# Cross attention with 16 heads: scores on two row tiles of 64 rows, rows built through memory

## The reference

```python
h = layernorm(x)                                   # [8, 256, 128]
q, k, v = split(h @ w_qkv.T)                       # 16 heads of 8 features
k = concat([context_k, k]);  v = concat([context_v, v])   # 512 + 256 = 768 keys
attn = softmax((q * 8 ** -0.5) @ k.T)              # per head [256, 768], fp32
x = x + (attn @ v) @ w_proj.T + b_proj
x = x + expert_ffn(layernorm(x))                   # 8 experts, 2 per row
```

## Time and profile before

| | us |
|---|---|
| median of 3 runs (lowest, highest) | 581.93 (579.75, 582.76) |
| the profiled execution, its own time | 579.1 |
| its span, first to last instruction | 577.5 |
| TensorE / VectorE / ScalarE / GpSimd busy | 498.9 / 353.9 / 292.7 / 196.0 |

### The profile page before, as it was taken

One profiled execution on the slowest core, in us unless ns is written; L12 is line 12 of the kernel. 1 busy time (PEld: TensorE's weight loads), 2 busy tenths in 40 slices (PEclk: granted clock), 3 DMA queues, 4 the chain that ended last, 5 costly groups with the idle time before them and its releaser, 6 DMA issues. The chain is left out here.

```text
span 577.5 us, 10586 instructions
## 1 busy us (share of the span) xinstructions
PE 498.9 (86%) x3467; PEld 322.9 (56%) x3468; DVE 353.9 (61%) x646; ACT 292.7 (51%) x584; POOL 196.0 (34%) x381
## 2 busy tenths in 40 slices
PE   3479999999999999999999998555499999999940
PEld 1346666666666666666565663244447666666630
DVE  7597687777777787777777770368524333333316
ACT  2136667767767677676776767421023333333310
POOL 7151241331422412411400000103317776677630
PEclk9999999999999999999999999865569999999995
DMA  6802434445244344342332300160101111111116
GB/s 168 185 25 72 94 88 108 95 105 134 75 113 121 87 120 104 91 115 64 76 72 58 90 3 2 36 184 0 14 10 43 41 41 38 39 36 43 42 51 189
DMA packets 32078, 44.39 MB, mean 77 GB/s; under 512 B 5484, under 2 KB 20460, under 8 KB 32036
## 3 DMA queue, kind: packets, MB, share of 16 engines
q1 hardware_dynamic: 27076, 36.88, 25.7%
q0 software_dynamic: 2560, 5.25, 3.6%
q10 hardware_dynamic: 2400, 1.70, 1.2%
HBM read 16.58 MB, written 4.72 MB: 37 GB/s over the span
## 5 line engine op out<-in xcount | busy, mean ns | idle before, releaser
L426 DVE TENSOR_REDUCE max_part<-max_ps 128x2 f32<-128x1024 f32 (+1 forms) x192 | 231.3, 1221 | 79.6 <-PE max_ps L519 42.1
L385 ACT ACTIVATE probs<-exp_ps 128x512 f32<-128x512 f32 x384 | 207.4, 591 | 77.5 <-PE exp_ps L541 72.0
L541 PE MATMUL exp_ps<-blocks,keys 128*128 128x512 f32 x384 | 160.9, 421 | 4.5 <-ACT probs L385 2.3
L519 PE MATMUL max_ps<-keys,blocks 128*128 128x512 f32 x256 | 109.9, 436 | 10.1 <-DMA blocks<-masked 7.0
L541 PEld LDWEIGHTS exp_ps<-blocks,keys 128*128 128x128 f32 x384 | 71.7, 187 | 44.8 <-ACT probs L385 18.5
L551 PE MATMUL pv_ps<-probs,value_cols 128*32 128x256 f32 x1536 | 96.3, 383 | 0.0
L986 DVE TENSOR_TENSOR hidden<-up_ps,silu 128x512 f32<-128x512 f32 x40 | 27.7, 692 | 84.4 <-PE up_ps L1076 82.4
L302 POOL CAST maxes<-rowmax 128x8 fp32r<-128x8 f32 x32 | 6.3, 198 | 178.6 <-DVE rowmax L432 178.6
L519 PEld LDWEIGHTS max_ps<-keys,blocks 128*128 128x128 f32 x256 | 48.4, 191 | 30.2 <-DVE max_part L426 19.2
L551 PEld LDWEIGHTS pv_ps<-probs,value_cols 128*32 128x32 f32 x1536 | 43.3, 109 | 39.4 <-issue 17.1
L879 ACT ACTIVATE hiddenT<-at_ps 128x512 f32<-128x512 f32 x40 | 23.9, 597 | 77.2 <-PE at_ps L1093 68.7
(11 more groups left out here) (148 smaller groups left out, 473.4 us busy)
## 6 DMA issues: line engine op xcount, KB each, us to landing
blocks<-masked SPq DMA_DIRECT2D x93, 128.0 KB
keys<-parts SPq DMA_DIRECT2D x96, 96.0 KB
ctx_v_sb<-ctx_v_dram SPq DMA_DIRECT2D x8, 256.0 KB, 2.9
gate<-gateT_dram SPq DMA_DIRECT2D x8, 256.0 KB, 2.8
up<-upT_dram SPq DMA_DIRECT2D x8, 256.0 KB, 2.6
y_in<-pick_outs SPq DMA_DIRECT2D x8, 256.0 KB, 4.9
raw<-ctx_kT_dram SPq DMA_DIRECT2D x7, 256.0 KB, 2.8
h_rows<-h SPq DMA_DIRECT2D x4, 256.0 KB, 4.9
```

The source lines that it names most:

```text
L385: act.activation(probs[par][:, k, 2 * half:2 * half + 2], exp_ps[u % 2][:].rearrange("p (g n) -> p g n", n=N), ACT.Exp).then_inc(exp_done, 1)
L426: vec.reduce_max(out, bank, axis=AX.X).then_inc(max_done, 1)
L519: mm = pe.matmul(max_ps[w % 2][:, half * BANK:(half + 1) * BANK], blocks[:, t, w, half * P:(half + 1) * P], keys[:, t, 0:NC_], start=True, ...
L541: pe.matmul(exp_ps[u % 2][:], keys[:, t, k * P:(k + 1) * P], blocks[:, t, 2 * half:2 * half + 2, :], start=True, stop=True).then_inc(exp_f ...
```

## The change

`keys` and `blocks` are laid out for two pairs of heads a quad. Pair a = 0 lies on partitions 0 to 49 and pair a = 1 on 64 to 113: three bands of 16 rows each (2 heads of 8 features) and two sum rows. A matmul takes 64 partitions (maxima: 48) in place of 128, and matmuls of the two pairs stand on different row tiles of the array. The number of score matmuls and their columns stay the same. In each group both halves of the maxima unit come first (a = 1, then a = 0), and then the exponential units for a = 0 and a = 1, each with a PSUM bank of its own. The maxima matmuls leave the sum rows out, so the clearing DMA goes.

SP writes the bands of a whole batch to DRAM by six DMAs (`write_bands`), and reads those of a quad back by four (`read_bands`). `parts` and `masked` have one buffer each in place of two. `masked`, its making and `blocks` are half as wide. The sum rows of a quad take two DMAs in place of one.

```diff
+PAIR = G // 2
+TILE = P // 2
+BAND = PAIR * D
+MAX_ROW = 3 * BAND
...
-        masked = sb("masked", [P, 2, 2, G, N])
+        masked = sb("masked", [P, 2, PAIR, N])
-        blocks = sb("blocks", [P, T, G, N], F32R)
+        blocks = sb("blocks", [P, T, PAIR, N], F32R)
+        key_bands = nc.dram_tensor("key_bands", (2, 2 * T, 3, BAND, KEYS), F32, kind="Internal").ap()
+        query_bands = nc.dram_tensor("query_bands", (2, 2 * T, 3, BAND, PAIR * N), F32, kind="Internal").ap()
...
-            def spread_rows(q):
+            def write_bands(c):
+                if c >= 2:
+                    for t in range(T):
+                        sp.wait_ge(rows_in[t], rows_spread(T * (c - 2)))
+                for j, part in enumerate((0, 1, 0)):
+                    sp.dma_start(key_bands[c % 2, :, j], parts_f[:, part, 0:KEYS]).then_inc(bands_in[c % 2], 16)
+                for j, part in enumerate((0, 0, 1)):
+                    sp.dma_start(query_bands[c % 2, :, j], masked[:, part]).then_inc(bands_in[c % 2], 16)
+
+            def read_bands(q):
                 c, t = divmod(q, T)
...
+                sp.wait_ge(bands_in[c % 2], bands_written(c))
+                for a in range(2):
+                    rows = slice(TILE * a, TILE * a + MAX_ROW)
+                    sp.dma_start(blocks_f[rows, t], query_bands[c % 2, 2 * t + a].rearrange("j i n -> (j i) n"))\
+                      .then_inc(rows_in[t], 16)
+                    sp.dma_start(keys_f[rows, t], key_bands[c % 2, 2 * t + a].rearrange("j i n -> (j i) n"))\
                       .then_inc(rows_in[t], 16)
...
-            sp.wait_ge(blocks_zero, T)
             sp.wait_ge(ctx_split, 2)
-            sp.wait_ge(own_first, 2)
-            spread_rows(0)
             sp.wait_ge(own_first, 4)
-            for q in range(1, T):
-                spread_rows(q)
+            write_bands(0)
+            sp.wait_ge(blocks_zero, 1)
+            sp.wait_ge(rows_const, 1)
+            for q in range(T):
+                read_bands(q)
...
                     sp.wait_ge(maxT_copied, s + 2)
                     q = (s + 1) % T
-                    sp.dma_start(blocks_f[SUM_ROWS:SUM_ROWS + 2, q], maxT_f[:, (s + 1) % 2, :]).then_inc(max_in[q], 16)
+                    for a in range(2):
+                        row = TILE * a + MAX_ROW
+                        sp.dma_start(blocks_f[row:row + 2, q], maxT_f[2 * PAIR * a:2 * PAIR * (a + 1), (s + 1) % 2, :])\
+                          .then_inc(max_in[q], 16)
+                if r == 0 and b + 1 < B and b >= 0:
+                    sp.wait_ge(ctx_split, 2 * (b + 1) + 2)
+                    sp.wait_ge(own_split, 4 * (b + 1))
+                    write_bands(b + 1)
...
                     sp.wait_ge(exp_filled, (s + 1) * XUNITS)
-                    spread_rows(s + T)
+                    read_bands(s + T)
...
-                pe.matmul(exp_ps[u % 2][:], keys[:, t, k * P:(k + 1) * P], blocks[:, t, 2 * half:2 * half + 2, :],
-                          start=True, stop=True).then_inc(exp_filled, 1)
+                pe.matmul(exp_ps[a][:], keys[rows, t, k * P:(k + 1) * P], blocks[rows, t], start=True, stop=True)\
+                  .then_inc(exp_filled, 1)
...
-                    for half in range(2):
-                        if has_scores(s + 2):
-                            max_half(s + 2, i, half)
-                        if has_scores(s):
-                            exp_unit(s, 2 * i + half)
+                    if has_scores(s + 2):
+                        max_half(s + 2, i, 1)
+                        max_half(s + 2, i, 0)
+                    if has_scores(s):
+                        exp_unit(s, 2 * i)
+                        exp_unit(s, 2 * i + 1)
```

More of the change, by code:

```diff
@@ L41 @@
 ROWS = 32
-SUM_ROWS = 3 * ROWS
 SCALE = float(D) ** -0.5
@@ L116, in attend @@
         bias_added = sem("bias_added")
+        bands_in = [sem(f"bands_in{i}") for i in range(2)]
         rows_in, max_in = [sem(f"rows_in{t}") for t in range(T)], [sem(f"max_in{t}") for t in range(T)]
@@ L161, in load_keysT, with mask_queries @@
             engine.dma_start(raw[:, c % 2, 0:NC_], d["ctx_kT"][c]).then_inc(keysT_in[c % 2], 16)
[L163 to L172, removed]
+        def mask_queries(engine, part):
+            spread = [P, PAIR, N]
+            return engine.tensor_tensor(masked[:, part],
+                                        parts_f[:, part, KEYS:KEYS + N].unsqueeze(1).to_broadcast(spread),
                                         mask[:].unsqueeze(2).to_broadcast(spread), ALU.mult)
-        rows_spread = lambda q: 16 * (6 + 7 * (q // T))
+        rows_spread = lambda q: 64 * (q // T + 1)
+        bands_written = lambda c: 96 * (c // 2 + 1)
         @block.sync
@@ L245, in split_context @@
                 pool.wait_ge(keysT_in[c % 2], 16 * (c // 2 + 1))
-                if c >= 2:
-                    for t in range(T):
-                        pool.wait_ge(rows_in[t], rows_spread(T * (c - 2)))
+                if c:
+                    pool.wait_ge(bands_in[(c - 1) % 2], bands_written(c - 1))
                 split(ctx_split, 2 * c, c, slice(0, NC_))
@@ L277, in _ @@
                                pattern=[[-1, P]], channel_multiplier=1).then_inc(ident_done, 1)
-            for t in range(T):
-                pool.memset(blocks[:, t].bitcast(F32), 0.0).then_inc(blocks_zero, 1)
+            pool.memset(blocks[:].bitcast(F32), 0.0).then_inc(blocks_zero, 1)
             split_context(0)
@@ L510, in project_values, with max_half @@
                 mm.then_inc(v_filled, 1)
[L512 to L514 removed]
+            def max_half(q, w, a):
+                t, rows = q % T, slice(TILE * a, TILE * a + MAX_ROW)
+                if w == 0 and a:
                     pe.wait_ge(rows_in[t], rows_spread(q))
[L516 removed]
+                if a:
                     wait_for(pe, max_done, q * MUNITS + w - 1)
                 if w < G:
[L519 to L520 removed]
+                    g, i = divmod(w, QT)
+                    mm = pe.matmul(max_ps[w % 2][:, a * BANK:(a + 1) * BANK], blocks[rows, t, g, i * P:(i + 1) * P],
+                                   keys[rows, t, 0:NC_], start=True, stop=True)
                 else:
                     for i in range(QT):
[L523 to L527 removed]
+                        first = a * BANK + i * N
+                        mm = pe.matmul(max_ps[w % 2][:, first:first + N], blocks[rows, t, w - G, i * P:(i + 1) * P],
+                                       keys[rows, t, NC_:KEYS], start=True, stop=True)
+                if a == 0:
                     mm.then_inc(max_filled, 1)
```

78 lines of the change are left out of this document (28 added, 50 removed).

## The result

The kernel with the change takes 666.88 us (median of 4 runs, 664.85 to 671.66), beside 582.35 for the kernel before on the same chip: a ratio of 1.147 (95% interval 1.1395 to 1.1549). Ratios and their intervals are taken without a version's slower executions, so they need not be the ratio of the medians shown. The forecast was 648, within 592 to 700, and slower with 0.88; its own case was to end between 628 and 664. The profiled execution took 668.5 us with a span of 666.7, so 89.2 us more than the span of before. The forecast had 66 of them.

A forecast was written before the change was run, and what follows sets the result against it. The prediction took a ring between TensorE and ScalarE to bound the kernel. Stalls 51, start 12 and pairs with tile forms 3 made 66 us on the profiled 579.1, so 645, and 648 as median; 8 in 10 range 592 to 700.

The forecast's parts named there:

- The forecast's case: Band writes at 150 GB/s stall batches 1 to 7 and delay the start: 648 us, range 628 to 664, chance 0.50.
- Landing of the writes: Each batch's six band writes, 1.97 MB at 150 GB/s: 13.1 us plus 1.8 us fixed, landed at 224.3.
- Length of the stall: TensorE waits 6.3 us at the first quad of batches 1 to 7; with the clock, 7 x 7.3 = 51 us.
- The predicted second step: Sum rows queue on SP behind the band wait: first exponential matmul 6.3 us late, where the maxima are 6.0 late.
- The clock, the term that was too small: TensorE runs at the lower clock after each stall: 1.0 us added per stall (0 to 2).
- Start: Batch 0's writes go out at 14.5 and quad 0's reads land at 33.6: first maxima matmul 12 us later.
- Pairs and forms: Score matmul pairs overlap, saving 6 us; changes of tile form on TensorE cost 9 us; net 3 us more.
- 16 us for full drains: Alternative price of the tile form changes, if each fully drained the array: 5 x 2 x 0.2 x 8 = 16 us.
- Wide writes: 590: Rival: band writes run at 303 GB/s, no stall or clock loss, start costs 5.4 us: 590 us, chance 0.12.
- Serial pairs: Rival: score pairs do not overlap, one more maxima matmul ahead of the exponential per value block: 14 us, 662, chance 0.14.
- TensorE's pace as the bound: Rival: TensorE's pace holds ScalarE and VectorE; halved score time gains 34 us, 553 with wide writes, chance 0.09.
- this ring: TensorE and ScalarE in the attention: ScalarE runs dry behind value blocks; two such rounds make about 10 us a quad.

The follow-up runs named there:

- their leaving out: The changed kernel with the band writes of batches 1 to 7 left out, all reads taking batch 0's bands: 619.59 us, ratio 1.0608 to the kernel before.
- the earlier writes: The changed kernel with the six band writes put ahead of the wait for the transposed maxima in SP's queue: 658.28 us, ratio 1.1289 to the kernel before.
- the wide version: The changed kernel with head rows outermost in DRAM, so a write's destination has 128 outer rows, not 8: 606.56 us, ratio 1.0343 to the kernel before.
- the order alone: The kernel before, on full tiles, with both maxima halves first and then both exponential units: 597.14 us, ratio 1.0248.
- the added pairs: The wide version with each maxima pair issued a second time into the same bank, behind the exponentials: 623.45 us in one run.
- the spread products on the wide version: The wide version with the value products 16, 8, 0, 8, 8, 8 by group instead of 24 behind groups 1 and 4: 583.62 us, ratio 0.9963.
- the three blocks: spread5_start with 16 value products behind groups 1, 3 and 5 instead: 590.39 us, ratio 1.0158 to the kernel before.
- spread5_start: The wide version with spread products, batch 0's context key columns written once split, and value_cols cleared ahead of blocks: 579.72 us, ratio 0.9933 to the kernel before.
- three traces with five blocks: The wide version with spread products: alone 583.62 us, with writes ahead of the sum rows 582.13 us, and spread5_start 579.72 us.

## Why the prediction was right, and where it was too small

- **Mechanism and forecast.** The forecast's case came: narrow writes, a stall on batches 1 to 7, a late start. Wide writes and their leaving out take the stall away, and the earlier writes only move it. The time lies above the range of that case, 628 to 664, and inside the wide one: the clock was mis-sized, and the shorter wait went the other way.
- **Landing of the writes**: 14.9 us predicted, 13.93 measured (13.84 at the start). Less the 1.8 taken as fixed that is 12.1 us, 162 GB/s for the 150 chosen. That it came so close is partly luck: in full flow the writes ran at 205 GB/s, above the 130 to 185 allowed, where 1.97 MB take 9.6 us, and some 4.3 us went beside it, where 1.8 were put in. The step from the 8 blocks to half the engines held; it is shown by the wide version.
- **Length of the stall**: 6.3 predicted, 5.6 measured, and 57.2 - 18.7 = 38.5 us in seven waits of TensorE. The faster writes won 1.0, a landing of 3.2 us instead of 2.65 took half of it back. The predicted second step, exponentials later than maxima through SP's queue, is there (0.21 us idle at 236.16) but hardly counts, because the maxima themselves ran at half pace by then.
- **The clock, the term that was too small.** This term of the sum was mis-sized: 1.0 us a stall was put in for four matmuls at the lower clock, and nothing for the quads behind it. Of 9.5 us a batch 5.5 are the wait and 0.4 the tile forms. The 3.6 that remain are put down to the clock: 0.50 for 4 us, 0.76 for 4 more, and again in the second quad, 11.6 us long, whose value block took 2.79 us at 200.06 where the usual takes 1.50. The estimate came from the start of the kernel before, where the doubled spacing ended within 4 us. At the start of this kernel, where row tiles follow, it lasted far longer: four small maxima matmuls took 0.80 us at 40.80, 6 us behind the first, where the usual four take 0.50 (208.01), and the value block at 58.90 still took 2.79. The clock column reads 1.00 at both starts, so it can't be relied on there.

```profile
40.80 0.80 PE L536 MATMUL max_ps<-keys,blocks 48*128 48x256 f32 x4 [0.34 <-DVE max_part L436]
...
58.90 2.79 PE L563 MATMUL pv_ps<-probs,value_cols 128*32 128x256 f32 x24
...
200.06 2.79 PE L563 MATMUL pv_ps<-probs,value_cols 128*32 128x256 f32 x24
```

- **The clock without a stall, which the prediction put at nothing.** About 4.6 us before the merge of the ninth quad (2.9 in the third quad, the one of the value block at 58.90) and 3.8 at the last value blocks. The last ones in order of time:

```profile
438.53 2.48 PE L563 MATMUL pv_ps<-probs,value_cols 128*32 128x256 f32 x24
...
445.22 2.79 PE L563 MATMUL pv_ps<-probs,value_cols 128*32 128x256 f32 x24
```

  Before, three such blocks at that place took 1.50, 1.50 and 1.65 us, with the clock at 1.00. The wide version, without stalls, has the same: its last merge comes 21.8 us later than before's, of which 6.2 are there at the first merge, 31 quads x 0.1 = 3 are the tile forms, and 12.5 are left: 2.8 in its third quad, where the value block at 51.46 took 2.79 us under a column of 1.00, and the rest in stretches like 165:175. The steady state's writes do not cause them, since the version without those writes has them; nor does the order alone. All traces on full tiles are free of them between 60 us and the last merge; of those on row tiles three are (the added pairs, the spread products on the wide version, and the three blocks) and the other six are not. So they go with row tiles, and what brings one on stays open.
- **Start**: 12 predicted, 13.3 measured by the first maxima matmul (34.82 against 21.55), 13.7 by the first merge. The writes went out at 16.20, not 14.5. "The half-size memsets ... are hidden" was wrong: GpSimd reached its memset of value_cols 0.7 us earlier (7.41, before 8.10), beside the first of VectorE's four normalizations of xn:

```profile
6.51 3.53 DVE L425 TENSOR_SCALAR xn<-x,ln_aggr_sb,ln_rstd_sb 128x128 f32<-128x128 f32 x4
```

```profile
7.41 1.98 POOL L298 MEMSET value_cols<- 128x2208 f32 x1
```

  In the kernel before the same four read 3.63 us (6.52), but there the memset met only the last of them, and the transposes that need the first of them started at 8.11; here they start at 9.69:

```profile
8.11 0.66 PE L497 MATMUL shared_ps<-ident,xn 128*128 128x128 f32 x2 [8.11 <-DVE xn L415]
```

```profile
9.69 0.66 PE L508 MATMUL shared_ps<-ident,xn 128*128 128x128 f32 x2 [9.69 <-DVE xn L425]
```

  With that memset moved ahead (spread5_start) the same four instructions took 1.71 us.
- **Pairs and forms**: the pairs overlap, and the net price is as predicted; the gain is not seen. The pair of exponentials behind a value block takes 0.40 us for two:

```profile
206.57 1.50 PE L563 MATMUL pv_ps<-probs,value_cols 128*32 128x256 f32 x24
208.01 0.50 PE L536 MATMUL max_ps<-keys,blocks 48*128 48x256 f32 x4
208.35 0.40 PE L553 MATMUL exp_ps<-blocks,keys 64*128 64x512 f32 x2
```

  ScalarE's gap behind a value block is 1.2 to 1.5 us. Both terms net were 0.4 us a batch; an undisturbed batch of the wide version is 42.0 against 41.6. But ScalarE waits 10.5 us for exponential matmuls in it (79.31:121.31), where it waited 8.8 before, so the 0.75 us that the order was to save are not in these waits. The two terms were not parted by a run. (The prediction's 16 us for full drains count 0.2 us each where the sentence names 0.4; the sum does not use them.)
- **The sum.** 66 predicted, 89.2 measured: start +1.7, stalls -0.8 x 7 = -5.6, clock behind stalls +2.6 x 7 = 18.2, clock without a stall +8.4, the rest 0.5. The clock's two terms are 26.6 us, more than the whole miss of 23.2; the shorter wait hid part of it, which is luck.
- **The rivals.** Wide writes: 590 was priced, 606.56 came for it, 17 too few. The profiled execution, 610.34, is 23 above its price of 587.5: 12.5 in the quads and 5 in the last value blocks, at the lower clock, 0.8 at the start, and 4 behind the attention that no run takes apart. Serial pairs: excluded by the trace, its price confirmed by the order alone. TensorE's pace as the bound: the spread products show a part of it, 2 us a batch or some 15 in all, and only with the products moved; the rest of the 23 us that they won lies in the clock and the last value blocks.

## What to carry to other kernels

Read a DMA's destination as the engines will share it: here 8 outer blocks ran at 205 GB/s and 128 at 389, and the layout with the partitions' rows outermost in memory cost the reads nothing and won 60 us. When a change makes TensorE's work smaller, price its clock too: this ring, whose pace ScalarE sets, gained nothing from lighter matmuls, and lost at times the granted clock that the heavier ones kept. Read the clock from the matmuls' own times as well as from its column. Moving a bulk transfer ahead of a small, urgent one on the same queue only moved the stall.

## What the runs showed of the hardware that was not expected

- The granted clock falls to 1.2 GHz (0.50) in an attention where nothing stalls (170:175 of the wide version), with matmuls of 48 and 64 rows, and with the value products spread as well (two of three traces with five blocks). It stayed at 2.4 GHz (1.00) in one execution with a fifth more matmuls, in one with three blocks, and with full tiles between 60 us and the last merge in either order. What exactly decides, these runs don't tell.
- Near the start the clock column reads 1.00 also where matmuls run at half pace: a value block took 2.79 us at 51.46 in the wide version, as at 200.06 of the change with the column at 0.50, against the usual 1.50.
- After a stall of 5.6 us the lower clock came back once more in the quad behind, not only right after the wait; the last of the seven stalls had no such second fall (a quad of 10.0 us behind it).
- With writes on their way SP takes longer to issue the next: 1.0 to 1.8 us for a narrow write in the mean of three, where a DMA of a calm stretch takes 0.42; and two small DMAs behind 2 MB of writes made TensorE wait up to 6.9 us.
- The same 2 MB to memory: 205 GB/s at a DMA share of 0.51, and 389 at 1.00.
- With a GpSimd memset of 128 x 2208 (1.98 us) beside them, four fp32 tensor_scalar instructions of 128 x 128 took 3.53 us, or 3.63 in the kernel before, against 1.71 without it.
